# Median search with its flags stored values innermost, its lower bound kept as a tally column, and the weight split re-placed

## What is computed

```python
def _L0_conv_ref(x, cfc_w, bn_w, bn_b):
    ...
    u = jnp.stack([mean, mx, std], axis=-1)
    med = jnp.median(u.reshape(b, -1), axis=-1)[:, None, None]
    u = (u - med) ** 3
    z = jnp.einsum('bck,ck->bc', u, cfc_w)
    z = z / jnp.sqrt(jnp.float32(1.0) + BN_EPS) * bn_w + bn_b
    return x * jax.nn.sigmoid(z)[:, :, None, None]
...
def step(prev, x_i):                      # layer 3, over the columns, forward and back
    y = jnp.einsum('oc,nch->noh', Wc, prev) + conv_b[None, :, None]
    y = jnp.where(y >= 0, y, prelu_a * y)
    cur = y + x_i
    return (cur, cur)
...
x = x + _L0_conv_ref(_gn(x), ...)         # _gn: group norm, 32 groups
x = x + _L1_conv_ref(_gn(x), ...)
x = x + _L2_conv_ref(_gn(x), ...)
x = x + _L3_conv_ref(_gn(x), ...)
```

## Time and profile before

| what | value |
|---|---|
| median of three runs | 969.11 us (968.66 to 970.0) |
| span of the profiled execution | 968.5 us |
| PE busy | 789.3 us, 81% |
| DVE busy | 758.7 us, 78% |
| ACT busy | 407.2 us, 42% |
| POOL busy | 31.2 us, 3% |
| granted TensorE clock | 0.997 of full speed |

### The profile page before, as it was taken

One profiled execution on the slowest core, in us unless ns is written; L12 is line 12 of the kernel. 1 busy time (PEld: TensorE's weight loads), 2 busy tenths in 40 slices (PEclk: granted clock), 3 DMA queues, 4 the chain that ended last, 5 costly groups with the idle time before them and its releaser, 6 DMA issues.

```text
span 968.5 us, 13873 instructions
## 1 busy us (share of the span) xinstructions
PE 789.3 (81%) x4087; PEld 633.5 (65%) x4087; DVE 758.7 (78%) x1536; ACT 407.2 (42%) x1349; POOL 31.2 (3%) x45
## 2 busy tenths in 40 slices
PE   0002222259999999999999999999999999999996
PEld 0001111148888888888888888888888888888885
DVE  7999898886777777777777777888888888888887
ACT  6950100004444444444444444444444444444444
POOL 1030220000000000000000000000000000000002
PEclk9999999999999999999999999999999999999998
DMA  9820110000000000000000001222222222222223
GB/s 355 363 65 22 44 44 1 1 1 1 0 0 0 0 0 0 0 0 0 0 0 0 0 0 43 87 87 87 87 87 87 87 87 87 87 87 87 87 87 108
DMA packets 71627, 54.74 MB, mean 57 GB/s; under 512 B 1984, under 2 KB 67520, under 8 KB 69568
## 3 DMA queue, kind: packets, MB, share of 16 engines
q1 hardware_dynamic: 71184, 54.53, 17.4%
q10 hardware_dynamic: 432, 0.07, 0.0%
HBM read 37.81 MB, written 16.78 MB: 56 GB/s over the span
## 4 chain that ended last, share of the span: by engine, by line
PE 78%; DVE 19%; issue 1%; DMA 1%; ACT 0%; DVEq 0%; ACTq 0%
PE ps_prods L405 24%; PE ps_prods L409 24%; PE ps_prods L408 24%; DVE less L554 8%; PE ps_turns L417 6%; DVE half_max L485 4%; DVE bn_parts L480 1%; PE ps_below L386 1%; DMA x_sb<-x_cols 1%; DVE few L569 1%; DVE cell L572 0%; DVE thr L578 0%; DVE t L467 0%; DVE rstd L469 0%; DVE t L468 0%
## 5 line engine op out<-in xcount | busy, mean ns | idle before, releaser
L405 PE MATMUL ps_prods<-w_hi,s_hi 128*128 128x512 f32 x992 | 402.8, 406 | 0.1
L408 PE MATMUL ps_prods<-w_lo,s_hi 128*128 128x512 f32 x992 | 401.4, 405 | 0.0
L409 PE MATMUL ps_prods<-w_hi,s_lo 128*128 128x512 f32 x992 | 391.4, 395 | 0.0
L351 ACT ACTIVATE act_buf<-ps_prods 128x256 f32<-128x256 f32 x248 | 82.1, 383 | 358.9 <-PE ps_prods L409 355.9
L655 DVE SCALAR_TENSOR_TENSOR x_sb<-act_buf,x_sb 128x256 f32 (+1 forms) x248 | 107.3, 433 | 156.8 <-ACT act_buf L357 146.1
L409 PEld LDWEIGHTS ps_prods<-w_hi,s_lo 128*128 128x128 f32 x992 | 187.3, 189 | 38.6
L405 PEld LDWEIGHTS ps_prods<-w_hi,s_hi 128*128 128x128 f32 x992 | 186.9, 188 | 38.8 <-DVE s_lo L645 0.9
L408 PEld LDWEIGHTS ps_prods<-w_lo,s_hi 128*128 128x128 f32 x992 | 187.6, 189 | 32.6
L357 ACT ACTIVATE act_buf<-ps_turns,bias 128x128 f32<-128x128 f32 x496 | 157.7, 377 | 50.7 <-PE ps_turns L417 50.7
L363 ACT ACTIVATE ps_below<-ps_turns,neg_bias 128x128 f32<-128x128 f32 x496 | 153.1, 362 | 0.0
L662 DVE SCALAR_TENSOR_TENSOR x_sb<-ps_below,neg_slope,x_sb 128x256 f32 (+1 forms) x248 | 119.4, 481 | 5.0
(11 more groups left out here) (96 smaller groups left out, 389.5 us busy)
## 6 DMA issues: line engine op xcount, KB each, us to landing
x_sb<-x_cols SPq DMA_DIRECT2D x16, 1024.0 KB, 21.3
stage<-x_cols SPq DMA_DIRECT2D x31, 512.0 KB, 4.1
out_cols<-x_sb SPq DMA_DIRECT2D x31, 512.0 KB, 4.8
stage<-w_t SPq DMA_DIRECT2D x16, 256.0 KB, 2.8
x_sb<-x_cols SPq DMA_DIRECT2D x1, 512.0 KB, 3.8
out_cols<-x_sb SPq DMA_DIRECT2D x2, 256.0 KB, 2.3
params<-gates ACTq DMA_DIRECT2D x1, 60.0 KB, 5.5
bias<-conv_bias ACTq DMA_DIRECT2D x1, 4.0 KB, 7.5
```

What stands on the lines that cost most here:

```text
L351: act.activation(act_buf[:, half], ps_prod[c][:, half], ACT.Copy).then_inc(raw_copied, 1)
L405: pe.matmul(ps_prod[c], s_hi[:, k, :], w_hi[:, k, w_cols], start=(k == 0), stop=False)
L408: pe.matmul(ps_prod[c], s_hi[:, k, :], w_lo[:, k, w_cols], start=False, stop=False)
L409: return pe.matmul(ps_prod[c], s_lo[:, k, :], w_hi[:, k, w_cols], start=False, stop=(k == CT - 1))
```

## The change

It does three things.

- The flags lie values innermost: the index in `less` is (n * marks + t) * 24 + s (`by_mark`). DVE's innermost loop now writes neighbours, and PE reads the 28 flags of one value with a step of 48 bytes. The parts become 5, 8 and 11 values (`PARTS = [0, 5, 13]`).
- `lo`, `base`, `cell` and their instructions (lines 560, 540) go. The flags of the counts are multiplied by the step of the round as they are made (`few`), and each row of them has one column more that holds the lower bound. One reduction over the row then gives the new lower bound, and it lands in the column of the other of two tally tiles; the marks of the next round are ticks times step plus that bound. After the last round one reduction over `last_tally` gives `floors` and takes the place of line 572 and line 581; a copy of the bound for the second rank stands between the last compares and the wait for the count.
- The weights are loaded whole, 8 transfers of 512 KB without a wait on SP, into `w_raw`, which lies in the same place as `w_lo`. ACT makes `w_hi` in 8 instructions of 128 x 1024 before the first gate. POOL subtracts half tile h in place, once the three compares of search round h are done: 8 halves in layer 0's rounds and 8 in layer 1's.

```diff
-    PARTS = [0, 11, 19]
+    STEP = [SEARCH_WIDTH / ARY ** (k + 1) for k in range(ROUNDS)]
+    PARTS = [0, 5, 13]
...
+        landing = ExitStack()
+        w_raw = landing.enter_context(nc.sbuf_tensor("w_raw", [P, CT, C], fp32))
+        landing.close()
         w_lo = sb("w_lo", [P, CT, C], fp32r)
...
+        def by_mark(k):
+            return less[:, 0:N * round_marks(k) * VALUES].rearrange("p (m s) -> p m s", s=VALUES)
...
-            for h in range(W_LOADS):
-                if h >= 2:
-                    sp.wait_ge(w_lo_done, h - 1)
-                sp.dma_start(stage_half(h), w_half(w_t, h)).then_inc(w_staged[h % 2], 16)
-            sp.wait_ge(w_lo_done, W_LOADS)
+            for ct in range(CT):
+                sp.dma_start(w_raw[:, ct, :], w_t[:, ct, :]).then_inc(w_loaded[ct], 16)
...
             for h in range(W_LOADS):
-                pool.wait_ge(w_hi_done, h + 1)
-                pool.tensor_tensor(w_half(w_lo, h), stage_half(h), w_half(w_hi, h).bitcast(fp32), ALU.subtract)\
+                pool.wait_ge(w_hi_done, h // 2 + 1)
+                pool.wait_ge(compared, (h + 1) * len(PARTS))
+                pool.tensor_tensor(w_half(w_lo, h), w_half(w_raw, h), w_half(w_hi, h).bitcast(fp32), ALU.subtract)\
...
-            split_w(W_LOADS // 2)
+            for ct in range(CT):
+                act.wait_ge(w_loaded[ct], 16)
+                act.activation(w_hi[:, ct, :], w_raw[:, ct, :], ACT.Copy).then_inc(w_hi_done, 1)
             for layer in range(LAYERS):
...
-                if layer == 0:
-                    split_w(W_LOADS // 2)
...
                         last = pe.matmul(ps_count[:, 0:N * marks], ones_bf[:, :],
-                                         less[:, s * N * marks:(s + 1) * N * marks],
+                                         by_mark(k)[:, :, s],
                                          start=(s == 0), stop=(s == VALUES - 1))
...
-                    below = less[:, 0:VALUES * N * marks].rearrange("p (s n t) -> p n t s", n=N, t=marks)
+                    below = by_mark(k).rearrange("p (n t) s -> p n t s", n=N)
...
-                    if k > 0:
-                        link(dve.scalar_tensor_tensor(lo[:, :], cell[:, 0, :], step * ARY, lo[:, :],
-                                                      ALU.mult, ALU.add))
-                    if not last_round:
-                        place_marks(base, step / ARY, lo, k + 1)
-                    dve.wait_ge(counted, layer * ROUNDS + k + 1)
...
+                    if k < ROUNDS - 1:
+                        few = tally[:, k % 2, :, :]
+                        dve.wait_ge(counted, layer * ROUNDS + k + 1)
+                        link(dve.tensor_scalar(few[:, :, 0:marks], counts, float(MEDIAN_RANK), STEP[k],
+                                               ALU.is_le, ALU.mult))
+                        low = tally[:, (k + 1) % 2, :, LOW:ARY] if k < ROUNDS - 2 else last_tally[:, 0, :, ARY:ARY + 1]
+                        link(dve.tensor_reduce(low, few, AX.X, ALU.add))
+                        place_marks(k + 1, low)
+                    else:
+                        dve.tensor_copy(last_tally[:, 1, :, ARY:ARY + 1], last_tally[:, 0, :, ARY:ARY + 1])
+                        dve.wait_ge(counted, layer * ROUNDS + k + 1)
+                        for upper in range(2):
+                            ins = dve.tensor_scalar(last_tally[:, upper, :, 0:ARY], counts, float(MEDIAN_RANK + upper),
+                                                    STEP[k], ALU.is_le, ALU.mult)
+                        link(ins)
+                link(dve.tensor_reduce(floors[:, :, :], last_tally[:, :, :, :], AX.X, ALU.add))
```

More of the change, by code:

```diff
@@ L90, in gated_norm_and_column_scan_kernel @@
         cube = tmp("cube", [P, N, NSTAT + 1, CT])
-        less = tmp("less", [P, VALUES * N * ARY], bf16)
+        less = tmp("less", [P, N * ARY * VALUES], bf16)
         params = tmp("params", [P, LAYERS, NSTAT + 2, CT])
@@ L97, in gated_norm_and_column_scan_kernel @@
         thr = tmp("thr", [P, N * ARY])
[L98 to L101, removed]
+        tally = tmp("tally", [P, 2, N, ARY])
+        last_tally = tmp("last_tally", [P, 2, N, ARY + 1])
         floors = tmp("floors", [P, 2, N])
@@ L140, in gated_norm_and_column_scan_kernel @@
         masks_ready = sem("masks_ready")
-        w_staged = [sem(f"w_staged{b}") for b in range(2)]
+        w_loaded = [sem(f"w_loaded{ct}") for ct in range(CT)]
         w_hi_done = sem("w_hi_done")
@@ L183, in w_half @@
             return tile[:, h // 2, (h % 2) * HALF:(h % 2 + 1) * HALF]
-        def stage_half(h):
-            return stage[:, (h % 2) * HALF:(h % 2 + 1) * HALF]
         def over_rows(v, cts=CT):
@@ L530, in median, with place_marks @@
                 values = unit[:, :, :, :].rearrange("p n k c -> p n (k c)")
-                def place_marks(out, step, start, k):
+                def place_marks(k, start):
                     marks = round_marks(k)
                     nth = ticks[:, 0:marks].unsqueeze(1).broadcast_to([P, N, marks])
-                    out = out[:, 0:N * marks].rearrange("p (n t) -> p n t", n=N)
+                    out = thr[:, 0:N * marks].rearrange("p (n t) -> p n t", n=N)
                     if isinstance(start, float):
-                        link(dve.tensor_scalar(out, nth, step, start, ALU.mult, ALU.add))
+                        link(dve.tensor_scalar(out, nth, STEP[k], start, ALU.mult, ALU.add))
                     else:
[L540 to L545, removed]
+                        link(dve.scalar_tensor_tensor(out, nth, STEP[k], start.broadcast_to([P, N, marks]),
+                                                      ALU.mult, ALU.add))
+                LOW = ARY - 1
+                dve.memset(tally[:, 0, :, LOW:ARY], SEARCH_LO)
+                place_marks(0, SEARCH_LO)
                 for k in range(ROUNDS):
                     marks = round_marks(k)
-                    last_round = k == ROUNDS - 1
-                    below = less[:, 0:VALUES * N * marks].rearrange("p (s n t) -> p n t s", n=N, t=marks)
+                    below = by_mark(k).rearrange("p (n t) s -> p n t s", n=N)
                     marked = thr[:, 0:N * marks].rearrange("p (n t) -> p n t", n=N)
@@ L557, in median @@
                                           ALU.is_lt).then_inc(compared, 1)
-                    if k > 0:
-                        link(dve.scalar_tensor_tensor(lo[:, :], cell[:, 0, :], step * ARY, lo[:, :],
-                                                      ALU.mult, ALU.add))
-                    if not last_round:
-                        place_marks(base, step / ARY, lo, k + 1)
-                    dve.wait_ge(counted, layer * ROUNDS + k + 1)
-                    ranks = 2 if last_round else 1
@@ L568, in median @@
[L568 to L580, removed]
@@ L581, in median @@
-                link(dve.scalar_tensor_tensor(floors[:, :, :], cell[:, :, :], step,
-                                              lo[:, :].unsqueeze(1).broadcast_to([P, 2, N]), ALU.mult, ALU.add))
+                    counts = ps_count[:, 0:N * marks].rearrange("p (n t) -> p n t", n=N)
+                    if k < ROUNDS - 1:
[13 more added lines that the diff above has]
+                        link(ins)
```

## The result

The changed kernel takes 914.77 us (914.71 to 914.88) against 968.9 us in the same comparison: 0.9436 times the time of before, 95% interval 0.9423 to 0.945, so 54.1 us less. The forecast was 914.1 us.

The account below looks back on a forecast made before the run. DVE's chain was taken to bound the searches, with PE working in its gaps. 968.5 - 46.0 (searches) - 9.8 (weight split) + 0.8 (POOL meetings) = 913.5 us span, plus 0.6 to the median: 914.1 us; range 908 to 930.

Parts of the forecast that it names:

- The compares: DVE's three compares in a search round: 1.05 ns a flag instead of 4.17, 1.00 us in place of 3.06.
- rival 4: Search compares: the layout brings nothing, 4.17 ns comes from narrow outputs as such; about 960 us; chance 0.03.
- PE's count: PE's strided count matmuls in a search round: 48 ns each, PE keeps up, last 11 end at 1.72 us.
- my own bound of 50 ns: Search rounds: where a count matmul takes over 50 ns, PE never catches up with the compares.
- rival 1: Search rounds: PE becomes the bound through costly strided reads; between 919 and 955 us; chance 0.15.
- the sign that I had named: PE's count in a round: a burst of 24 matmuls without a gap would show the forecast wrong.
- The last round: Last search round, from the compares' start to line 585: 2.51 us instead of 4.73, line 581's 0.2 us gone too.
- The marks: Three linked DVE instructions after the count: still 0.67 us a round; lines 560 and 540 set nothing.
- The weight split outside the search: POOL's subtractions leave the stretches before layer 0's search (6.1 us) and between layers 0 and 1 (3.7): 9.8 us less.
- POOL in the rounds: Placing of marks held by POOL's subtraction for 0.05 us in 16 rounds: 0.8 us more, bounds 0 and 10.
- rival 3: Search rounds: POOL also holds reductions or `few`, or its instruction grows; up to 10 us back, 923 us; chance 0.10.
- ACT and SP: Weight loads and ACT's 8 instructions cost nothing; the last tile lands at about 62 us, ACT ends by 66.

Follow-up runs that it names:

- the control with parts of 8: Kernel with flags 8 bytes apart and POOL's work in 24 pieces, its six compares joined to three of 8, 8 and 8 values: 906.74 us, ratio 0.9339.

## Why the prediction was right, and where it was not

- **The compares.** 1.05 ns a flag and 1.00 us a round were forecast; 0.99 to 1.00 us were measured. The layout did what it says, rival 4 is out.
- **PE's count.** The step that did not hold is that PE keeps up and rests before the last 11 matmuls. The price of a strided matmul was nearly right, 48 ns forecast and 51 measured, just over my own bound of 50 ns. What tips it is the arrival of the second part: I had it at 0.62 us, the end of its compare, without the 0.06 us of handing over that the first and the last part had. It is 0.68, and from there eight matmuls end at 1.06 even at 48 ns, past the last part's 1.05. A single matmul with the strided read also takes 0.23, not 0.19 us. So PE starts the last 11 at 1.08 instead of 1.05, they take 0.04 us longer, and the last of them another 0.04: PE's end comes 0.11 us late, at 1.83. The state of a round is that of rival 1, at its lower end; the sign that I had named, a burst of 24 without a gap, is there but for the short wait for the second part. That the time was only 0.7 us off is in part luck: 0.11 us too little for PE's burst met 0.07 us too much for the start of `few`; 2.50 against 2.54 us a round. Without the second error the forecast would have been 1.7 us lower, 912.4 us, and the measured time would still lie within its range.
- **The last round** was to be 2.51 us and is 2.64. I had taken its matmuls at the 48 ns of 28 flags; with 32 flags they are 58 ns.
- **The marks.** I priced the tally column at line 581's 0.2 us a layer and took the removal of lines 560 and 540 at nothing, because they lie in the wait for PE. They do, but the wait on base's semaphore cost 0.06 us a round behind it. The whole part is worth 2.2 us, not 0.6.
- **The weight split outside the search.** 6.1 + 3.7 us forecast, 12.4 - 6.3 and 14.4 - 10.7 measured: the same.
- **POOL in the rounds.** 0.8 us forecast, nothing measured: rounds with and without a subtraction are equal. I took the time from the placing's start to POOL's end as lost. But a held placing ends 0.04 us after POOL, and an undisturbed one takes 0.19 us anyway; so nothing is lost where it starts less than about 0.15 us before POOL's end, an estimate from these two numbers. Measured are 0.09 and 0.12 us before it at no cost (the changed kernel and the control with parts of 8) and 0.18 at 0.03 us. That rival 3 is out is shown by the reductions beside POOL; that the held placing is a real cost is shown by the kernel with flags 8 bytes apart.
- **ACT and SP** cost nothing, as said; the weights landed by 57 us and not at 62. The DMA engines had room for them in the load stage: their busy share there is 0.95 now and was 0.75 before.
- **The sum.** Searches 61.1 us (60.0 + 0.8 forecast), outside 9.8 less (9.8). The scan, from its first product to the end, is 0.7 us shorter in the profiled span, while the median lies 1.8 instead of 0.6 us above the span; the two nearly cancel. Neither is a gain or a loss of the change. The time of one execution lies 1.7 to 1.8 us above its own span in every run with both numbers, and the scan, the same code everywhere, took 754.6 to 756.9 us in the traces. The 0.6 us in the sum compares the span of one execution with the median of others; by the 1.7 to 1.8, an estimate, the profiled execution of the kernel before took about 970.3 us, a little over its median.

## What to carry to other kernels

Where one engine writes a tile and another reads it across, neither has to take the full stride: blocks of 4 bf16 values (8 bytes) let DVE write at 1.05 ns an element and PE read at its usual rate. Together with POOL's shorter pieces that gave 10 us more than moving the whole stride from DVE to PE. When one engine of a chain gets faster, look at what the other now meets: the subtraction on POOL was free only while PE was slow, and had to be cut into shorter pieces to cost nearly nothing (0.03 us a round). So a part of a change has no price of its own: the new split was worth 7.9 us alone and 14.5 beside the new layout. Before you read a group in the timeline as running without a gap, look at when its single instructions start. An instruction that is hidden in a wait is not free if the engine has to wait for it by a semaphore as well.

## What the runs showed that I had not expected

- PE reads one bf16 flag per 16 bytes or more at about 1.8 ns each (28 flags: 49 to 52 ns a matmul, 32 flags: 58 ns), and not slower at 64 bytes than at 16; at 8 bytes a matmul of 28 columns follows the last after 27 ns, as with neighbours.
- DVE's write of single bf16 flags 56 bytes apart costs 4.17 ns each, but in runs of 4 it costs the same as in one piece.
- A DVE wait on PE that stands behind another, already fulfilled wait starts its instruction about 0.06 us later; an instruction in that place without a wait does not.
- A DVE instruction with two SBUF inputs that is held by POOL's subtraction ends 0.04 us after it, whether it started 0.58 us before POOL's end (it takes 0.62) or 0.18 us (0.22).
- POOL's subtraction takes 0.91 us for 341 columns and 1.26 for 512: 2.05 ns a column and 0.21 us fixed.
